# Key stages of a two-step graph attention kernel: column chunks, keys inside the mix, last block's affine step

## The reference, cut to what matters

```python
R = adj + eye(N);  R = R / R.sum(-1, keepdims=True)
Z, Xf, Xa = 0, x, x
for n in range(2):
    q = Xa @ W1.T @ W2.T;  k = Xa @ W3.T        # 64 features
    probs = softmax(q @ k.T)
    A = probs, kept in each row until the sorted sum reaches 0.9, renormalized
    Xf = R @ Xf
    Xa = A @ Xa
    Z = Z + Xf @ U1[n].T + Xa @ U2[n].T
h = layernorm(x + Z) * ln_g + ln_b
out = layernorm(x + h)
```

## Time and profile before

| what | value |
|---|---|
| times of three runs | 1726.5, 1723.66, 1725.13 us; median 1725.13 |
| the profiled execution | 1724.79 us, of which 1723.2 us is the span of its core |
| mean granted TensorE clock | 0.947 of full speed |
| PE, DVE, ACT, POOL busy | 89%, 78%, 46%, 13% of the span |

### The profile page before, as it was taken

One profiled execution on the slowest core, in us unless ns is written; L12 is line 12 of the kernel. 1 busy time (PEld: TensorE's weight loads), 2 busy tenths in 40 slices (PEclk: granted clock), 3 DMA queues, 4 the chain that ended last, 5 costly groups with the idle time before them and its releaser, 6 DMA issues. The chain is left out here.

```text
span 1723.2 us, 17953 instructions
## 1 busy us (share of the span) xinstructions
PE 1536.2 (89%) x4753; PEld 886.1 (51%) x4753; DVE 1338.1 (78%) x3740; ACT 786.3 (46%) x1245; POOL 232.6 (13%) x267
## 2 busy tenths in 40 slices
PE   6999999977999999998999999994267979888995
PEld 3555555434555555554565555563134545444553
DVE  4788888746677777776899999998878888896562
ACT  3555555312555556554444444442223435334443
POOL 1010210212000000000011111123110211212322
PEclk9999999988999999999999999996588989999997
DMA  6456666552455555555566666750000000000000
GB/s 236 170 169 148 152 172 198 139 220 94 176 189 189 188 190 194 201 201 208 195 159 173 181 165 185 193 170 1 2 3 0 1 7 7 7 1 7 7 7 12
DMA packets 52652, 211.92 MB, mean 123 GB/s; under 512 B 22048, under 2 KB 30816, under 8 KB 31952
## 3 DMA queue, kind: packets, MB, share of 16 engines
q1 hardware_dynamic: 49296, 210.59, 39.1%
q0 software_dynamic: 3264, 0.30, 0.2%
HBM read 206.63 MB, written 4.48 MB: 123 GB/s over the span
## 5 line engine op out<-in xcount | busy, mean ns | idle before, releaser
L1663 DVE MAX8 cand<-psL 128x8 f32<-128x256 f32 (+1 forms) x640 | 372.8, 584 | 60.6 <-PE psL L858 49.4
L1217 ACT ACTIVATE psL<-psL,umax 128x1024 f32<-128x1024 f32 x256 | 278.5, 1088 | 298.6 <-DVE umax L1657 295.1
L857 PE MATMUL psL<-kA,mq 128*128 128x512 f32 x512 | 301.1, 588 | 8.0 <-DVE mq L1483 8.0
L828 PE MATMUL psO<-adj_in,xn 128*128 128x512 f32 x512 | 242.5, 596 | 4.5 <-DMA adj_in<-in_adjT 2.8
L1033 PE MATMUL psO<-ebuf,xn 128*128 128x512 f32 x512 | 241.7, 594 | 0.0
L828 PE MATMUL psO<-adj_in,xf 128*128 128x512 f32 x512 | 240.7, 594 | 0.0
L1928 DVE SCALAR_TENSOR_TENSOR ebuf<-ebuf 128x1024 f32<-128x1024 f32 x128 | 156.7, 1225 | 98.7 <-PE psO L1033 93.5
L1363 ACT ACTIVATE ebuf<-psL 128x1024 f32<-128x1024 f32 x128 | 130.0, 1022 | 188.5 <-PE psL L1070 134.1
L858 PE MATMUL psL<-kB,mq 66*128 66x512 f32 x512 | 204.5, 399 | 0.0
L1320 ACT ACTIVATE ebuf<-psL 128x1024 f32<-128x1024 f32 x128 | 131.1, 1024 | 132.7 <-PE psL L1005 132.5
L1082 PE MATMUL psO<-xf,xa 128*128 128x512 f32 x340 | 167.1, 615 | 17.6 <-DVE xf L2130 17.6
(11 more groups left out here) (354 smaller groups left out, 2053.2 us busy)
## 6 DMA issues: line engine op xcount, KB each, us to landing
adj_in<-in_adjT SPq DMA_DIRECT2D x128, 1024.0 KB, 4.9
adj_in<-in_adj SPq DMA_DIRECT2D x32, 2048.0 KB, 7.6
xaT<-in_xT SPq DMA_DIRECT2D x1, 2048.0 KB, 7.7
xa_dram<-xa SPq DMA_DIRECT2D x8, 256.0 KB, 7.8
out<-t SPq DMA_DIRECT2D x8, 256.0 KB, 2.3
list_dram<-ids,place POOLq DMA_INDIRECT x64
rel_prob<-cut_dram SPq DMA_DIRECT2D x32, 2.0 KB
cut_dram<-ncut SPq DMA_DIRECT2D x16, 2.0 KB
```

What stands on the lines that cost most here:

```text
L828: last = nc.tensor.matmul(psO[:], fs[:, j, :], adj_in[:, r % RING, j % JQ, :], start=(j == 0), stop=(j == JT - 1))
L857: nc.tensor.matmul(o, qA[:, t * P:(t + 1) * P], kA[:, c:c + BI], start=True, stop=False)
L1217: nc.scalar.activation(ps[:], ps[:], ACT.Exp, bias=umax[:, bass.ds(i * UB + k, 1)], scale=1.0, accum_out=usum[:, bass.ds(i * UB + k, 1)]). ...
L1663: last = v.max(cand[:, t % 2, at + c * 8:at + c * 8 + 8], psL[(turn + k) % 3][:, c * WIDE:(c + 1) * WIDE])
```

## The change

Six edits of order and of who does what; what is computed is the same.

1. The load of xT is split into four column chunks with a semaphore each, and TensorE's key units of step 0 wait for their own chunk. The sync queue waits for the second chunk before it issues xn and what follows. LOADS_FIRST falls to 4.
2. kB is no longer a second copy by ScalarE from PSUM but a copy by GpSimd from kA, in both steps, ahead of GpSimd's self adds.
3. Key units and the first query are brought forward and interleaved: in step 0 the query comes behind unit 0, and the first logits need the keys of units 0 to 2 only.
4. The flow of step 0 starts three units later (FLOW_FROM), in six windows over the 125 units left; the wait for the remaining weights moves there. The semaphores of the adjacency ring are shared by both steps.
5. The first query of step 1 is made inside block 7 of the first mix, key units 0, 1 and 2 of step 1 between its last weighs (they need only rows of blocks 0 to 5), and key unit 3 after the first two logits units of the second rank stage.
6. In the sweep the last block's gain, shift and addition of x (the affine part) is done by VectorE, and the tile preparation at the end of a round is put ahead of the last block's centrings on ScalarE: the tile's copies before the first, its exponentials before the second.

The diff, cut to its core:

```diff
@@ sync queue
-            for dst, src in ((w1_sb[:], w1), ..., (wk[:, DA:P], w3T), (xaT[:], xT)):
+            for dst, src in ((w1_sb[:], w1), ..., (wk[:, DA:P], w3T)):
                 sp.dma_start(dst, src).then_inc(loaded_first, 16)
+            for u in range(NU):
+                sp.dma_start(xaT[:, u * UNIT:(u + 1) * UNIT], xT[:, u * UNIT:(u + 1) * UNIT]).then_inc(xt_in[u], 16)
+            sp.wait_ge(xt_in[1], 16)
@@ flow windows
+        FLOW_FROM = 3
         def flow_window(a):
-            return a * NB * UB // FLOWS, (a + 1) * NB * UB // FLOWS
+            units = NB * UB - FLOW_FROM
+            return FLOW_FROM + a * units // FLOWS, FLOW_FROM + (a + 1) * units // FLOWS
+        def k_bank(u):
+            return (0, 2, 1, 0)[u]
@@ GpSimd, each step
+                for u in range(NU):
+                    c = slice(u * UNIT, (u + 1) * UNIT)
+                    pool.wait_ge(g["k_act"], u + 1)
+                    nc.gpsimd.tensor_copy(kB[0:DA, c], kA[0:DA, c]).then_inc(g["k_pool"], 1)
@@ GpSimd, scaled
-                        add_rows(r, i)
+                        if i < NB - 1:
+                            add_rows(r, i)
@@ TensorE
+                if s == 0:
+                    for u in range(NU):
+                        pe.wait_ge(xt_in[u], 16)
+                        if u == NU - 1:
+                            pe.wait_ge(g["k_dve"], 1)
+                        k_unit(g, u)
+                        if u == 0:
+                            first_q(g)
...
+                            if prev is None and k < NU:
+                                pe.wait_ge(g["k_dve"], NU - 1 if k < 2 else NU)
+                                pe.wait_ge(g["k_pool"], max(k + 1, NU - 1) if k < 2 else NU)
...
+                                if i * UB + k == FLOW_FROM:
+                                    pe.wait_ge(loaded, 16 * LOADS)
...
                                     else:
+                                        pe.wait_ge(S[0]["m_yt_sb"], NB)
+                                        k_unit(g, NU - 1)
                                         pe.wait_ge(S[0]["xf_scaled"], NB)
@@ TensorE, end of the first mix
-                    for u in range(MU - LAG, MU):
-                        weigh(NB - 1, u)
-                    pe.wait_ge(g["m_yt_sb"], NB - 1)
+                    k_unit(S[s + 1], 0)
+                    weigh(NB - 1, MU - 2)
+                    pe.wait_ge(g["m_exp_done"], NB * MU)
+                    k_unit(S[s + 1], 1)
+                    k_unit(S[s + 1], 2)
+                    weigh(NB - 1, MU - 1)
+                    pe.wait_ge(S[s + 1]["r_q_lo2"], 1)
                     mix_to_rows(NB - 1)
@@ ScalarE
-                    nc.scalar.copy(kA[:, c], psL[u % 3][:])
-                    nc.scalar.copy(kB[0:DA, c], psL[u % 3][0:DA, :]).then_inc(g["k_act"], 1)
+                    nc.scalar.copy(kA[:, u * UNIT:(u + 1) * UNIT], psL[k_bank(u)][:]).then_inc(of["k_act"], 1)
@@ ScalarE, end of the first mix
+                    for u in range(NU - 1):
+                        k_hi(S[s + 1], u)
                     mix_o_copy(NB - 1)
                     xaT_copy(NB - 1)
                     for n in range(MU - NAT_LAG, MU):
                         add_rows(NB - 1, n)
+                        if n == MU - NAT_LAG + 2:
+                            k_hi(S[s + 1], NU - 1)
@@ ScalarE, end of a round of the sweep
                         mix_o_copy(r, NB - 1)
-                        centre(r, NB - 1, 0)
-                        centre(r, NB - 1, 1)
                         tile_rows_copy(r, PT + 1)
                         tile_q_hi(r, PT + 1)
+                        centre(r, NB - 1, 0)
                         for n in range(NU):
                             ...
                             tile_exp(r, PT + 1, n, w % 3, r * SW + AHEAD + w + 1)
+                        centre(r, NB - 1, 1)
@@ VectorE, end of the first mix
+                    k_lo(S[s + 1], 0)
+                    k_lo(S[s + 1], 1)
                     attend_y(NB - 1)
+                    k_lo(S[s + 1], 2)
                     for n in range(MU - NAT_LAG, MU):
                         add_rows(NB - 1, n)
+                    k_lo(S[s + 1], NU - 1)
                     scale_rows(NB - 1)
@@ VectorE, end of a round of the sweep
+                    def last_rows(r):
+                        arrived(g["centred"], r * NB + NB)
+                        link(v.tensor_tensor(t1[:], t1[:], gain..., ALU.mult))
+                        link(v.tensor_tensor(t1[:], t1[:], shift..., ALU.add))
+                        link(v.tensor_tensor(t1[:], t1[:], xn[:, (NB - 1) * TB:NB * TB, :], ALU.add))
                         z_add(r, NB - 1)
                         spread(yn)
-                        normed_spread(r, NB - 1)
                         tile_q_lo(r, PT + 1)
+                        last_rows(r)
+                        spread(t1)
                         tile_begin(r, PT + 1, ...)
```

More of the change, by code:

```diff
@@ L274, in gnn_kernel @@
         loaded_first = sem("loaded_first")
+        xt_in = [sem(f"xt_in{u}") for u in range(NU)]
         ready = sem("ready")
@@ L284, in gnn_kernel, with adj_loads @@
         stored = sem("stored")
+        adj_arrived = [sem(f"adj_in_{k}") for k in range(RING)]
+        def adj_loads(s, i, r):
+            return ((s * NB + i) * (PARTS // RING) + r // RING + 1) * 16
         def step_sems(s):
-            names = ["k_ps", "k_act", "k_dve"]
+            names = ["k_ps", "k_act", "k_dve", "k_pool"]
             names += ["r_q_ps", "r_q_hi", "r_q_lo", "r_q_hi2", "r_q_lo2", "r_l_ps", "r_exp_done", "r_o_sb"]
@@ L304, in step_sems @@
             signals = {name: sem(f"{name}{s}") for name in names}
-            signals["adj_in"] = [sem(f"adj_in{s}_{k}") for k in range(RING)]
+            signals["adj_in"] = adj_arrived
             if s == 0:
@@ L340, in flow_parts @@
             first, end = flow_window(a)
+            if unit < first:
+                return a, range(0)
             before = max(unit - first - 1, 0) * JT // (end - first - 1)
@@ L771, in _, with k_unit, first_q @@
                 xs, fs = features(s), flows(s)
-                if s > 0:
-                    pe.wait_ge(S[s - 1]["m_yt_sb"], NB)
-                for u in range(NU):
-                    if u >= 3:
-                        pe.wait_ge(g["k_dve"], u - 2)
+                def k_unit(of, u):
                     for hb in range(2):
-                        last = nc.tensor.matmul(psL[u % 3][:, hb * BI:(hb + 1) * BI], wk[:],
+                        last = nc.tensor.matmul(psL[k_bank(u)][:, hb * BI:(hb + 1) * BI], wk[:],
                                                 xaT[:, (2 * u + hb) * BI:(2 * u + hb + 1) * BI], start=True, stop=True)
-                    last.then_inc(g["k_ps"], 1)
+                    last.then_inc(of["k_ps"], 1)
+                def first_q(of):
+                    nc.tensor.matmul(psQ, wq[:], xaT[:, cols(0)], start=True, stop=True).then_inc(of["r_q_ps"], 1)
+                if s == 0:
[6 more added lines that the diff above has]
+                            first_q(g)
                 def to_rows(i):
@@ L838, in adj_with @@
                         return range(sum(counts[:k]), sum(counts[:k + 1]))
-                    if prev is None:
-                        pe.wait_ge(loaded, 16 * LOADS)
                     pe.wait_ge(g["r_q_lo"], i + 1)
@@ L1330, in mix_block @@
                                 mix_q_hi(i + 1)
+                            if not more and u == slot(11, MU):
+                                first_q_hi(S[s + 1])
                     def mix_q_hi(i):
@@ L1697, in rank_block @@
                                 q_lo(g["r_q_hi2"], g["r_q_lo2"], i, TB - 1, TB)
[L1699 to L1700 removed]
+                if s == 0:
+                    for u in range(NU):
+                        k_lo(g, u)
+                        if u == 0:
+                            first_q_lo(g)
+                else:
                     link(v.memset(hqB[DA:DA + 2, :].bitcast(FP32), 0.0))
[L1702 to L1703 removed]
                 for i in range(NB):
[L1705 removed]
+                    rank_block(i, i - 1 if i > 0 else None, i < NB - 1, (i + 1) % 3)
                 for n in range(SORTS):
@@ L1940, in mix_block @@
                                 mix_q_lo(i + 1)
+                            if not more and u == slot(12, MU):
+                                first_q_lo(S[s + 1])
                     link(v.memset(cutB[DA:DA + 1, :], 0.0))
```

60 lines of the change are left out of this document (34 added, 26 removed).

## The result

The changed kernel takes 1711.76 us (median of 4 runs, 1710.79 to 1714.31), the kernel before 1724.39 (4 runs, 1723.59 to 1726.5) beside it: ratio 0.9925, 95% interval 0.9912 to 0.9938. The forecast was 1705.5 with a range of 1702 to 1712. So direction and range held, the range by 0.24 us, and a third of the expected gain is missing. The profiled execution took 1711.07 us, its span 1709.4, against 1723.2: 13.8 us less, where the sum had 19.7.

What follows compares the result with a forecast made beforehand. TensorE paces both rank stages, so only three seams can gain: 8.0 + 1.5 + 10.2 = 19.7 us off the profiled 1724.8 gives 1705.1, median 1705.5. Range 1702 to 1712.

Steps and rivals of the forecast that it cites:

- the three seams: Before the first logits, between first mix and second rank stage, behind the last weigh: gains of 8.0, 1.5 and 10.2 us.
- late loads together with slow copies: Combined case of late loads and slow GpSimd copies that set the range's upper end, 1712.
- The tail's sum: End of the kernel: last centring done at 1710.1, store landed at 1712.7, span end 1713.0 instead of 1723.2, 10.2 us gained.
- The start's terms: Before the first logits: they come at about 17.2 instead of 25.60, 8.4 us, of which 8.0 is taken.
- the quarters: Start: the four chunks of xT's load land at about 7.0, 8.2, 9.5 and 10.9 us.
- The moved wait: Start: sync queue issues xn at about 8.2, not 3.95; costed at nothing, 4.3 us if xT's cover is gone.
- The second seam: First mix to second rank stage: flow starts at 799.2, not 802.38, fourth unit's logits at 805.3, not 806.99; 1.5 us gained.
- copies at the two-input pace: Rival, start and second seam: GpSimd copies take 2.4 us, total gain 17.4, 1707.7 us; chance 0.17.
- The loads gave back: Rival, start: quarters land together at 11.0, or xn and all behind it 4.3 us later; 1709.5 us; chance 0.15.
- TensorE did stay at the full level: Rival: TensorE stays at the full clock level through the second seam, 1.9 us more gained, 1703.6 us; chance 0.12.
- GpSimd was not starved: Slower rival: VectorE starves GpSimd, a copy takes 8.6 us and the kernel 1736.1 us; chance 0.03.
- The start's gain: Rival: it is lost wholly as first units wait for something unseen, 11.7 us left, 1713.4 us; chance 0.03.

Runs made afterwards that it cites:

- The order alone: Kernel before with only the tile's preparation put ahead of the last block's centrings, affine part left on GpSimd: 1721.32 us, one execution.
- the added work: Changed kernel with three unused 128x512 products more on GpSimd behind its last instruction: 1717.95 us, ratio 0.9958.
- the removed roots: Changed kernel with the last block's reciprocal roots on VectorE instead of GpSimd: 1713.43 us, ratio 0.9928.
- the affine part alone: Kernel before with only the last block's three affine operations on VectorE, order of the tail left: 1722.87 us, one execution.
- the tail put back: Changed kernel with the tail as in the kernel before, start and second seam still changed: 1719.26 us, ratio 0.9961.
- the long fillers: Changed kernel with eight unread products in TensorE's idle time at the start, each two matmuls of 0.44 us: 1717.85 us, ratio 0.9962.
- ScalarE's copies: Changed kernel with the copies for the keys' low part back on ScalarE, out of PSUM, instead of GpSimd: 1714.53 us, one execution.
- the packed seam: Changed kernel with the second seam reordered: late row sums between key copies, earlier adjacency load, fourth key unit ahead of first logits: 1708.81 us, ratio 0.9902.

## Why the prediction was right, and where its sum was off

**The direction held** because the gain does lie in the three seams, and the second rank stage kept what it was given (7.35 us from 807 to 1169). **The range held by luck:** its upper end was made of late loads together with slow copies. Neither came. What took the time instead stood nowhere in it, GpSimd's closing (4.1 us) and the loss in the first mix (1.6 us), and the median lies 0.24 us inside.

**The tail's sum failed at its last term:** "Then the store ... 1712.7, plus the 0.5 us between the last instruction and the end of span." All before it was right: the centring's end to 0.1 us, the affine steps, the store's landing (2.6 us against 2.7). The 0.5 us was read from a trace in which VectorE ended last. (Added up, the terms give 1713.2, not the 1713.0 that the sum went on with.) GpSimd's closing takes 8.53 us, and was there to be seen in the trace of before, hidden by 4 us; with the tile's preparation moved ahead and the centring chain at the end, that cover was gone. That costs 4.1 us and was no rival either: I asked what is late next among the instructions of the timeline, and the engines' closing isn't among them. The order alone, the added work and the removed roots agree with it and not with the store as the end; the affine part alone fits both. The tail was gained by the order (4.1 us) and by the affine part, which moves GpSimd's last instruction up by another 2.0 us.

**The start's terms:** the quarters land 0.8 us later than forecast (7.83, not 7.0; the forecast's own terms give 7.15), unit 0 takes 3.75, not 3.5, and the first query, at the lower level too, about 0.3 more than costed; together they are the 1.4 us by which the first logits miss 17.2. GpSimd's copies take 1.03, not 1.4, which frees nothing. The moved wait was costed at nothing; the diagonal add was 1.2 us late in this pair (0.4 in the means given above), and the fifth unit hid all but 0.5 of it. At the end of the stage 7.8 of the 8.0 were there. That the sum came so close is partly luck: it held the clock's dip of before (0.66 at 25 to 35 us) for the normal case and none for after. The three other traces with the old start had 0.83 there and end the stage at 324.90 to 325.95, against which the changed kernel's 318.64 is 6.3 to 7.3 us earlier. With a dip the new start gave 5.4.

**The second seam** went as summed. Add the 6.2 us of head start that after has there, and the last weigh ends at 787.5 (forecast 787.2), the fourth key unit begins at 793.5 (793.1), xf is scaled at 799.0 (798.5), the load is issued at 792.8 (792.6). One term is off: the diagonal add began 0.4 us late and took 2.22 us instead of 1.69, and with it flow starts at 800.3, not 799.2, and the fourth unit's logits at 805.9, not 805.3. But 1.1 us is no fixed worth. Four traces with this seam gained 1.1 to 1.2 us, that with the tail put back lost 0.6, that with the long fillers 0.5 and that with ScalarE's copies 1.8; of three with the seam of before, two moved by 0.07 at most and the one with the order alone lost 1.65.

**The first mix's 1.6 us** was in no term. Between the last exponential of the first rank stage and the exponential of the mix's seventeenth unit, the ten traces with the new start lost 1.3 to 2.4 us against the kernel before, but for the one with long fillers (0.4); the three with the old start lost 0 to 0.4. So it comes with the change, although no edit lies there. In the changed kernel the clock falls and rises about 1 us later against the work than before (the tile's logits reach the full level only at their last matmul, not at their third from the end), and the mix then begins at the lower level. But that is not the whole cause: two traces with the old start begin the mix at the lower level too and lost 0.4, and the one with the packed seam begins it at the full level and had lost 1.3 by then, with a granted clock of 0.57 from 326 to 330 us where the changed kernel has 1.00. The head start differed, 4.4 to 8.0 us, and the loss didn't follow it. What in the change moves the clock there stays open. The Trainium skill, TensorE: Matmul & The Clock Gate, Part 1, calls the point at which the level changes variable from run to run. At the start the traces agree (the same program had 1.00 and 0.68 at 25 to 35 us); here they don't, the loss is regular.

**The rivals:** copies at the two-input pace fell with 1.03 us. The loads gave back at most 1.2 us at the diagonal add, not 4. TensorE did stay at the full level for the logits of the second seam (785.34, 0.47 and 0.40 us a matmul) and fell afterwards (0.87 at 790 to 795 us). GpSimd was not starved: 1.03 to 1.04 us in all four copies beside VectorE, and two copies back to back in the packed seam took 2.01 us. (That rival's 1736.1 leaves out the 0.3 us that the other sums add.) The start's gain was not lost.

## What to carry to other kernels

Before the end of a kernel is shortened, list each engine's own closing with its start and its length: an engine that seems long done can be the next to end last, and its last instruction is then on the critical path whatever it computes. When a stage starts earlier, compare the granted clock of the gaps in both traces, not only the durations: differences of 1 to 3 us at a seam went with the clock's level, and in the one trace with them short matmuls that fit the gaps, of a kind whose price was read from the trace, kept it up. And a wait that ends a seam is worth following back through the queue that issues the load: here two row sums behind key copies held it for 8.8 us. Short is not enough for a filler: those that outlasted their gaps cost 3.4 us in the trace and 6 in the median.

## What the runs showed of the hardware

- GpSimd's DRAIN at the program's end took 8.53 us in thirteen of fourteen traces and 8.40 in the other (the one with added work), from its own last instruction on, also where that lay 25 us ahead of the end. VectorE's and SyncE's took 0.007 to 0.017 us, ScalarE's 1.1 to 2.4, TensorE's 1.5 to 3.5.
- GpSimd casts 64x1024 with one input in 1.03 us, 1.0 ns a column, as fast as ScalarE (1.01) and faster than VectorE's two-input step of the same size (1.23). The Trainium skill, GPSIMD Engine Reference, section 3.1, has 512 elements in 769 ns, an estimate of 1.5 us for 1024; the measurement decides, 1.03. The Trainium skill's rule in section 4.1, that one input runs near line-rate, fits better than the half of VectorE in its section 3.
- A product of 128x512 with x in full fp32 is two matmuls in the trace, 0.9 us in all at the full clock; one with the rounded key and query operands is 0.24.
